# A product that is multiplied ahead of, or behind, the maxima of its slot

## The reference

```python
Q = (x_text @ Wq).reshape(Bb, Tt, H, DH)        # 1024 tokens, H = 4 heads, DH = 32
K = (x_vision @ Wk).reshape(Bb, Gg, H, DH)      # 6404 context rows
scores = jnp.einsum('bthd,bghd->bhtg', Q, K) / np.sqrt(DH).astype(np.float32)
topv, topi = jax.lax.top_k(scores, K_TOP)       # K_TOP = 32 of 6404, for each token and head
probs = jax.nn.softmax(topv, axis=-1)
attn = jnp.zeros_like(scores).at[bi, hi, ti, topi].set(probs)
attn_mean = attn.mean(axis=1)                   # over the 4 heads
c_t = jnp.einsum('btg,bgd->btd', attn_mean, x_vision @ Wv)
```

## Time and profile before

| stretch of the profiled execution | us |
|---|---|
| search alone (slots 0 to 60) | 641 to 699 |
| search and weighting together (slots 61 to 415) | 699 to 1207 |
| one tile in it: product 0 of piece u = 4, tile 2 to tile 3 | 870.74 to 945.73 |
| weighting alone (the rest) | 1207 to 1268 |
| whole span: VectorE busy | 1291.5 (74%) |
| whole span: TensorE busy | 1406.3 (81%) |
| whole span: ScalarE, GpSimd busy | 935.3 (54%), 697.0 (40%) |

### The profile page before, as it was taken

How to read it: one execution, slowest core, us unless ns; L and a number is a source line. 1 busy time by engine, 2 the same in 40 slices (tenths; PEclk the granted TensorE clock), 3 DMA queues, 4 the chain that set the end, 5 groups by cost and what they waited for, 6 DMA issues and landing times. The chain is left out here.

```text
span 1734.2 us, 19964 instructions
## 1 busy us (share of the span) xinstructions
PE 1406.3 (81%) x6613; PEld 727.6 (42%) x6669; DVE 1291.5 (74%) x3068; ACT 935.3 (54%) x1467; POOL 697.0 (40%) x529
## 2 busy tenths in 40 slices
PE   5777799899986746889898898988858439999798
PEld 2223344333343511355454454545546324333365
DVE  5998577756427549999999999999857666676433
ACT  4665212557520310888888888888831236666321
POOL 0664312022000000789998988989820030000012
PEclk9799899999987867999999999999988658999899
DMA  6000110000019220000000000000020120000000
GB/s 146 1 1 0 39 55 36 0 1 0 0 27 204 55 64 1 1 1 1 1 1 1 1 1 1 1 1 1 1 84 15 28 75 1 1 1 1 1 0 13
DMA packets 30969, 37.37 MB, mean 22 GB/s; under 512 B 13889, under 2 KB 24096, under 8 KB 29732
## 3 DMA queue, kind: packets, MB, share of 16 engines
q1 hardware_dynamic: 29312, 24.19, 5.1%
q10 hardware_dynamic: 1544, 11.79, 3.3%
HBM read 29.73 MB, written 6.24 MB: 21 GB/s over the span
## 5 line engine op out<-in xcount | busy, mean ns | idle before, releaser
L1499 PE MATMUL psum<-film_ka,film_context_qa 97*128 97x512 bf16 (+1 forms) x832 | 322.6, 389 | 93.5 <-DVE search_and_weigh_e L1733 39.3
L1703 DVE MAX8 search_and_weigh_kept<-psum 128x8 f32<-128x171 f32 (+2 forms) x1216 | 331.4, 327 | 1.7 <-PE psum L1501 1.5
L1885 ACT ACTIVATE search_and_weigh_e<-psum,search_and_weigh_bias 128x512 f32<-128x512 f32 (+1 forms) x416 | 268.4, 666 | 59.7 <-PE psum L1501 55.4
L1501 PE MATMUL psum<-film_kb,film_context_qb 128*128 128x512 bf16 (+1 forms) x777 | 298.0, 385 | 0.0
L1733 DVE SCALAR_TENSOR_TENSOR search_and_weigh_e<-psum,film_context_top,search_and_weigh_e 128x512 f32<-128x512 f32 (+1 forms) x283 | 200.6, 716 | 13.4 <-ACT search_and_weigh_e L1885 11.7
L1756 POOL TENSOR_TENSOR search_and_weigh_e<-search_and_weigh_e,search_and_weigh_keep 128x512 f32<-128x512 f32 (+1 forms) x133 | 150.6, 1133 | 108.5 <-ACT search_and_weigh_keep L1864 105.3
L1499 PEld LDWEIGHTS psum<-film_ka,film_context_qa 97*128 97x128 bf16 x832 | 85.7, 103 | 241.8 <-DVE search_and_weigh_e L1733 104.5
L1760 POOL TENSOR_TENSOR search_and_weigh_mean<-search_and_weigh_e 128x512 f32<-128x512 f32 (+1 forms) x104 | 133.4, 1283 | 11.5 <-DVE search_and_weigh_e L1733 4.4
L1790 PEld LDWEIGHTS psum<-ctx_rows,search_and_weigh_mean_T 128*128 128x128 f32 (+1 forms) x816 | 122.7, 193 | 30.4 <-issue 4.1
L2997 POOL TENSOR_TENSOR residual<-residual,top_expert_kept 128x1024 f32<-128x1024 f32 x7 | 16.4, 2350 | 295.8 <-DVE top_expert_kept L2954 295.8
L1765 POOL TENSOR_TENSOR search_and_weigh_mean<-search_and_weigh_mean,search_and_weigh_e 128x512 f32<-128x512 f32 (+1 forms) x104 | 128.0, 1230 | 8.2
(11 more groups left out here) (548 smaller groups left out, 2658.0 us busy)
## 6 DMA issues: line engine op xcount, KB each, us to landing
film_kb<-film_k_rows ACTq DMA_DIRECT2D x4, 1601.0 KB
film_ka<-film_k_rows ACTq DMA_DIRECT2D x3, 1601.0 KB
ctx_T<-in_ctx_T SPq DMA_DIRECT2D x1, 2401.5 KB
gqa_experts_w<-in_L_ffn_W SPq DMA_DIRECT2D x1, 2048.0 KB
film_convolve_back<-in_dft_back SPq DMA_DIRECT2D x1, 1728.0 KB, 12.8
film_k_rows<-cross_attention_film_hi SPq DMA_DIRECT2D x6, 256.0 KB, 2.1
film_k_rows<-cross_attention_film_mid SPq DMA_DIRECT2D x6, 256.0 KB, 2.0
film_k_rows<-cross_attention_film_low SPq DMA_DIRECT2D x6, 256.0 KB, 2.0
```

What stands on the lines that cost most here:

```text
L1499: pe.matmul(out, a["qa"][0:ROWS, h, rows], a["ka"][0:ROWS, h, c + b:c + b + cols], start=True, stop=False)
L1501: last = pe.matmul(out, a["qb"][:, h, rows], a["kb"][:, h, c + b:c + b + cols], start=False, stop=True)
L1703: last = dve.max(kept[:, h % 2, first + s, :], bank[:, lo:hi])
L1885: act.activation(e[:, n % RING, sub, 0:PIECES[u][1]], ps[:, SEARCH_BANKS + q % WEIGH_BANKS, 0:PIECES[u][1]], ACT.Exp, bias=bias[:, i % 2, ...
```

## The change

In every slot of VectorE the block with the product (and, in the last tile, the addition of heads 2 and 3) moves from the end of the slot to its beginning, ahead of the maxima, the picks and the limits. Nothing in it is altered, and no other engine's queue is.

```diff
         for G in range(STEPS + LAG + 1):
             for sub in range(NH):
+                n, h = divmod(NH * (G - LAG) + sub - MASK_LAG, NH)
+                if 0 <= n < STEPS and masked_on_vector(n, h):
+                    i, u = divmod(n, NCH)
+                    w = e[:, n % RING, h, 0:PIECES[u][1]]
+                    dve.wait_ge(e_ready, NH * n + h + 1)
+                    dve.scalar_tensor_tensor(out=w, in0=weigh_bank(n, h),
+                                             scalar=a["top"][:, NH * i + h, TOP - 1:TOP], in1=w,
+                                             op0=ALU.is_ge, op1=ALU.mult).then_inc(w_ready, 1)
+                    if h == NH - 1 and last_tile(n):
+
+                        dve.wait_ge(w_ready, masks_done(n + 1))
+                        other = e[:, n % RING, h - 1, 0:PIECES[u][1]]
+                        dve.tensor_tensor(other, other, w, ALU.add).then_inc(summed_ready, 1)
                 r = NH * G + sub
                 head, after = r // NCH - 1, r % NCH
                 picking = searching and 0 <= head < NT * NH and after < PICKS // 2
...
                         dve.tensor_tensor(least[:, i % 2, :], top[:, :, TOP - 1], b,
                                           ALU.add).then_inc(bias_ready, 1)
-                n, h = divmod(NH * (G - LAG) + sub - MASK_LAG, NH)
-                if 0 <= n < STEPS and masked_on_vector(n, h):
...
-                        dve.tensor_tensor(other, other, w, ALU.add).then_inc(summed_ready, 1)
```

## The result

The changed kernel took 1761.8 us (median of four runs, 1760.5 to 1762.7), the kernel before 1733.6 (four runs beside them, 1729.9 to 1734.8). The ratio is 1.0166, with a 95% interval of 1.0148 to 1.0183: slower by 28 us. The forecast was 1766, in a range of 1748 to 1787.

What follows compares the result with a forecast made beforehand. VectorE, busy 97%, was taken as the bound; new waits of 5.7 us a tile less today's 1.2, over 7 tiles, gave 31, plus 2 at limits, minus 1 at the last: +32 us, 1766 as median, range 1748 to 1787.

Steps and rivals of the forecast that it cites:

- u = 3 to 4: Steps 3 to 4 of a tile: VectorE waits 1.5 for exponential 120 and 0.8 for 121, sum 2.3 us.
- u = 5 to 6: Steps 5 to 6 of a tile: VectorE waits 0.6 for exponential 128 and 0.5 for 129, sum 1.1 us.
- u = 9 to 10: Steps 9 to 10 of a tile: VectorE waits 1.3 for exponential 144, then 0.5, sum 1.8 us.
- u = 7: Heads 1 of step 7 in a tile: by the same count, a new VectorE wait of 0.3 us.
- u = 1: Heads 0 of step 1 in a tile: by the same count, a new VectorE wait of 0.2 us.
- limits, head 1 of u = 12: At a tile's limits, VectorE's product 153 meets a new wait of 0.75 us for its exponential.
- limits, next tile's first: Behind the limits, the first exponential of the next tile may cost VectorE 0.2 us.
- The covers: Behind u = 1, 7 and 11, two or three pick slots give 1.6 to 2.4 us against some 1.5 needed; costed at nothing.
- The cover holds: Rival, chance 0.06: TensorE no longer waits for products, so exponentials come as much earlier as products; no change, 1734 us.
- Faster: Rival, chance 0.05: earlier products free banks and feed GpSimd sooner, VectorE's idle time shrinks; 1722 us at best.
- Slower still: Rival, chance 0.11: waits at the covered steps too, or low-clock spells from longer TensorE rests; 1789 us by the bound.
- saved spell: TensorE's 1.2 GHz spell behind the first tile's limits; by the skill's rule saved, sum 1.5 us lower; not taken.

Runs made afterwards that it cites:

- short masks (3): Changed kernel with the second activation (Relu) of ScalarE's masks left out, part of the computation changed; 1736.1 us, 1.0005 against the kernel before.
- weighting piece first (4): Changed kernel with TensorE's two units of a slot exchanged, weighting piece ahead of search piece; 1733.5 us, 1.0001 against the kernel before.
- both (9): Changed kernel with the second mask activation left out and TensorE's weighting piece ahead of its search piece; 1716.4 us, 0.9895 against the kernel before.
- kernel 6: Kernel before with the product in front only in slot 3 of the limits' step, where VectorE waits for the logarithm; 1730.6 us, ratio 1.0001.
- kernel 10: Changed kernel with every product one search piece earlier still, behind the maxima of q + 59; 1901.1 us, 1.0960 against the kernel before.

## Why the prediction was right

**The step that decided.** It was that the product comes one search piece earlier while its exponential comes hardly earlier, since weighting piece 117 stands behind a search piece that waits for the maxima of piece 175. It can be checked at its own anchor. In the changed kernel those maxima end at 873.65 (872.83 and the 0.82 of three of them), and exponential 120 began at

```profile
879.26 0.68 ACT L1885 ACTIVATE search_and_weigh_e<-psum,search_and_weigh_bias 128x512 f32<-128x512 f32 x1
```

so it ended 6.3 us after the maxima. The prediction said 6.4, and 4.87 for what VectorE has to do meanwhile: 1.5 of waiting, against 1.00 + 0.28 of idle time and 0.16 more, explained below. TensorE's rows show no wait from that search piece (873.71) to weighting piece 119, done at 877.14; exponential 119 begins right behind it, and then ScalarE is busy until exponential 120:

```profile
877.18 0.69 ACT L1885 ACTIVATE search_and_weigh_e<-psum,search_and_weigh_bias 128x512 f32<-128x512 f32 x1
```
```profile
877.58 0.10 PEld L1499 LDWEIGHTS psum<-film_ka,film_context_qa 97*128 97x128 bf16 x1 [0.22 <-DVE search_and_weigh_kept L1716]
```

The second row is TensorE's one wait for another engine in between, for the maxima of piece 178. It holds weighting piece 120, but that is done at 878.42, before ScalarE is free for it.

The same interval was read in the experiments, and it tells all four cases apart:

| kernel | maxima 175 to the end of exponential 120 | less 4.87 | idle ahead of product 120 (and 117) |
|---|---|---|---|
| changed | 6.3 | 1.4 | 1.28 |
| short masks (3) | 5.6 | 0.7 | 0.72 |
| weighting piece first (4) | 5.4 | 0.5 | 0.50 |
| both (9) | 4.8 | -0.1 | none |

So two things in series make the exponential late, TensorE's order and ScalarE's masks, each worth 0.7 to 0.9 us here, and either alone gives back part of it or all (3 and 4), both together everything (9). Kernel 4 still waits 0.50 and 0.69 at u = 4; its time came back over the whole tile, as told there. The prediction had named the first ("TensorE's own order (search first) keeps it behind the maxima") and counted the second in its 1.86 us between exponentials; my theory behind experiments 3 and 4 kept only the second, and fell.

**The terms.** In tile 2, as forecast and as measured (idle, and 0.08 for each wait):

| place | forecast | measured |
|---|---|---|
| u = 3 to 4 | 2.3 | 0.28 + 1.00 + 0.69 + 0.24 = 2.2 |
| u = 5 to 6 | 1.1 | 0.50 + 0.36 + 0.16 = 1.0 |
| u = 9 to 10 | 1.8 | 1.14 + 0.36 + 0.16 = 1.7 |
| u = 7 | 0.3 | 0.27 + 0.08 = 0.35 |
| u = 1 | 0.2 | 0.14 + 0.09 + 0.16 = 0.4 |
| limits, head 1 of u = 12 | 0.75 | 0.70 + 0.08 = 0.8 |
| limits, next tile's first | 0.2 | 0.28 + 0.08 = 0.36 |

The 0.08 is an overlap lost: the maxima of 876.71 were through at 878.98 and the product began at 879.97, 1.00 later by the view; without a wait it would have begun at 876.71 + 3 x 0.73 = 878.90, inside the end of the row before. Idle time under-reads each of these waits by that much.

The covers held. No wait of the tile stands behind two picked slots; the 0.69 of u = 4 and the 0.14 of u = 1 stand at the front of the first pick slot, ahead of its picks, and 0.09 behind it. u = 2 and 8, the steps behind u = 1 and 7, have none, and u = 12, behind u = 11, only that of the limits.

**The sizes.** The mixed stretch was forecast at 31 + 2 = 33 and took 30.0. Two terms were mis-sized. The first is the limits: the wait of 0.75 and the 0.2 came, and the logarithm's 0.66 went, as forecast, but small operations there got cheaper by 0.38 us a tile, which I had not looked at (last section), and the +0.3 became nothing. The second is the waits of before: the prediction took off their idle time, 1.2 in a tile, but counted the new ones from start to start. Tile 2 had four of them (0.61, 0.36, 0.17 and 0.06); with 0.08 each they are 1.5, so 0.3 too little came off in each of 7 tiles. With both put right the sum is 29. The last tile's limits and what follows were forecast at -1 and gave -2.8. Of this, 1.6 lies ahead of the last tile's first product (12.4 us for 14.0): the logarithm's wait fell from 1.40 to 1.00, and the subtraction of line 1729 took 0.29 us there for 1.11; one product of 0.65 also moved out into the mixed stretch. These are not the whole account, since other waits there changed as well. The other 1.2 lies in the weighting alone and was not followed further. In sum +32 was forecast and +28 measured.

**The rivals.** *The cover holds* is out by the tile: TensorE's waits for products did vanish, as that rival wanted, but gave the exponentials only 0.3 us at u = 4 (6.58 to 6.29 behind the maxima) and 0.6 at u = 6 (4.27 to 3.68), less than the 0.73 by which the product moved. *Faster* is out: the exponentials that would have had to end early are those VectorE waits for. The saving that the prediction saw at the limits is there in place (kernel 6 takes 2.4 us of waiting away) and too small to measure. *Slower still* is out for this distance, and is what one search piece further brings (kernel 10).

On the clock: the stretch has 0.99 before and after, and the search piece's 1.5 us wait did not come again. But the low clock did. From 720 to 1190 us it fell once before, behind the first tile's limits, and at three other places after. The first row is before, the others after; the clock is the third number from the end:

```profile
772.00:776.00 4.00, 4.00 (x15) 2.63 (x14) 4.00 (x14) 2.55 (x5) 3.77 (x5) 0.50 0.00 0
```
```profile
804.00:812.00 8.00, 6.88 (x29) 3.69 (x30) 8.00 (x28) 4.42 (x8) 7.61 (x7) 0.79 0.00 0
852.00:860.00 8.00, 7.15 (x35) 4.27 (x33) 7.29 (x22) 7.91 (x15) 6.72 (x7) 0.79 0.00 0
932.00:936.00 4.00, 3.29 (x9) 1.49 (x10) 3.90 (x13) 3.96 (x7) 3.77 (x4) 0.58 0.00 0
```

So the saved spell that the prediction worked out by the rule of the Trainium skill is not what the trace shows. VectorE waited for no search piece in these spells, and the 1.5 us went without it.

## What to carry to other kernels

An instruction that waits in an in-order queue is placed by two distances, to the work that it must follow and to the work that hangs on it; moving it is costed by following its input back to the last thing that the moving engine itself released, and counting what this engine still has to do from there. Do that count at every place of the period, since the loss sat at a few heads behind two masks and was hidden wherever picks gave cover. When the input is late, ask which engine's order puts other work ahead of it: exchanging two pieces in TensorE's queue gave back the 28 us, to within 3, and was worth nothing in the order that did not need it.

## What was not expected of the hardware

VectorE's operations of 128 x 4 elements take from 0.14 to 1.17 us each, and one of 128 x 128 from 0.28 to 1.20. The lines of the limits, first before and then after, 720 to 1190 (busy us, mean ns):

```profile
L1726 DVE TENSOR_TENSOR search_and_weigh_least<-film_context_top,search_and_weigh_bias 128x4 f32<-128x4 f32 x6 | 6.6, 1106 | 0.2
L1724 DVE TENSOR_TENSOR search_and_weigh_bias<-search_and_weigh_total,film_context_top 128x4 f32<-128x4 f32 x6 | 6.0, 992 | 4.0 <-ACT search_and_weigh_total L1894 4.0
L1716 DVE TENSOR_TENSOR search_and_weigh_shifted<-film_context_top 128x128 f32<-128x128 f32 x6 | 4.6, 774 | 0.0
...
L1725 DVE TENSOR_SCALAR search_and_weigh_bias<-search_and_weigh_bias 128x4 f32<-128x4 f32 x6 | 1.0, 170 | 0.2
```
```profile
L1729 DVE TENSOR_TENSOR search_and_weigh_shifted<-film_context_top 128x128 f32<-128x128 f32 x6 | 7.1, 1176 | 0.0
L1738 DVE TENSOR_SCALAR search_and_weigh_bias<-search_and_weigh_bias 128x4 f32<-128x4 f32 x6 | 7.0, 1169 | 0.2
...
L1739 DVE TENSOR_TENSOR search_and_weigh_least<-film_context_top,search_and_weigh_bias 128x4 f32<-128x4 f32 x6 | 1.0, 163 | 0.2
L1737 DVE TENSOR_TENSOR search_and_weigh_bias<-search_and_weigh_total,film_context_top 128x4 f32<-128x4 f32 x6 | 0.9, 148 | 0.0
```

The same four operations cost 3.04 us a tile before and 2.66 after, and which of them are the long ones has changed. What goes with it is GpSimd. In the two traces, all 22 operations of 128 x 4 at the limits that began while an instruction of GpSimd ran took 0.67 to 1.17 us and ended 0.02 behind that instruction; the 26 that began while none ran took 0.14 to 0.17. One of the long ones is at 920.40, 1.00 us to 921.40; beside it stood, to 921.38,

```profile
920.12 1.26 POOL L1760 TENSOR_TENSOR search_and_weigh_mean<-search_and_weigh_e 128x512 f32<-128x512 f32 x1
```

The 13 subtractions that began so ended 0.15 to 0.23 behind GpSimd's instruction. The sum (a reduction, with one input) took 0.26 to 0.29 either way. The subtraction of the last limits shows both cases: before, VectorE's row and GpSimd's beside it,

```profile
1212.64 1.11 DVE L1716 TENSOR_TENSOR search_and_weigh_shifted<-film_context_top 128x128 f32<-128x128 f32 x1
```
```profile
1212.45 1.16 POOL L1756 TENSOR_TENSOR search_and_weigh_e<-search_and_weigh_e,search_and_weigh_keep 128x512 f32<-128x512 f32 x1
1213.69 1.27 POOL L1760 TENSOR_TENSOR search_and_weigh_mean<-search_and_weigh_e 128x512 f32<-128x512 f32 x1
```

and after,

```profile
1242.09 0.29 DVE L1729 TENSOR_TENSOR search_and_weigh_shifted<-film_context_top 128x128 f32<-128x128 f32 x1
```
```profile
1240.76 1.28 POOL L1760 TENSOR_TENSOR search_and_weigh_mean<-search_and_weigh_e 128x512 f32<-128x512 f32 x1
1242.12 1.39 POOL L1764 TENSOR_TENSOR search_and_weigh_e<-search_and_weigh_e 128x512 f32<-128x512 f32 x1
```

Before, it began while GpSimd's multiplication ran (to 1213.61) and ended at 1213.75, just behind it. After, it began at 1242.09 between two of GpSimd's (1242.04 and 1242.12), took 0.29, and GpSimd's addition took 1.39 for its usual 1.23 to 1.27. This fits the Trainium skill, SBUF — State Buffer, section Who interferes with whom, which says that VectorE and GpSimd share a pair of ports by an exclusive lock, for a VectorE operation with two inputs in SBUF or in a two-port mode, and that whoever issues second blocks. The ends of all these rows agree with it. No run here took GpSimd's work away to test it, so that the ports are the reason stays that page's word.
